# The feed-forward input's two float16 halves: made from rows in SBUF and turned by DMA transposes, in place of TensorE transposes through PSUM

## What is computed

```python
x = _layernorm(x + attn(x), axis=-1)        # x: (4, 512, 512)
x = _layernorm(x + ffn(x), axis=-1)

def ffn(x):                                 # w1, w2: (1408, 512), w3: (512, 1408)
    x1 = x @ quantize(w1).T
    x2 = x @ quantize(w2).T
    return (sigmoid(x1) * x2) @ quantize(w3).T
```

## Time and profile before

| | us |
|---|---|
| median of 3 runs | 715.89 |
| lowest, highest | 715.37, 715.91 |
| span of the profiled execution | 713.9 |
| TensorE busy | 643.5 |
| VectorE busy | 493.3 |
| ScalarE busy | 352.4 |
| GpSimd busy | 129.6 |

### The profile page before, as it was taken

One profiled execution on the slowest core, in us unless ns is written; L12 is line 12 of the kernel. 1 busy time (PEld: TensorE's weight loads), 2 busy tenths in 40 slices (PEclk: granted clock), 3 DMA queues, 4 the chain that ended last, 5 costly groups with the idle time before them and its releaser, 6 DMA issues.

```text
span 713.9 us, 10940 instructions
## 1 busy us (share of the span) xinstructions
PE 643.5 (90%) x3336; PEld 351.8 (49%) x3336; DVE 493.3 (69%) x816; ACT 352.4 (49%) x814; POOL 129.6 (18%) x147
## 2 busy tenths in 40 slices
PE   6756667569999999999999999999999999997996
PEld 2534445243455655543565655644555565643442
DVE  2857878494887888557887886648887885654333
ACT  2664549251376767421576766411676675403320
POOL 1146450832200030012100210012000300110001
PEclk9686868879999999999999999999999999998999
DMA  7651514001122112002042030012032020010001
GB/s 259 236 184 27 195 29 149 0 1 30 29 54 88 38 43 76 1 34 83 7 119 56 6 90 29 17 49 60 16 105 60 9 51 1 16 45 0 1 1 59
DMA packets 20515, 42.02 MB, mean 59 GB/s; under 512 B 4704, under 2 KB 5856, under 8 KB 19936
## 3 DMA queue, kind: packets, MB, share of 16 engines
q1 hardware_dynamic: 19488, 39.86, 18.5%
q10 hardware_dynamic: 960, 1.33, 0.5%
HBM read 20.20 MB, written 4.19 MB: 34 GB/s over the span
## 4 chain that ended last, share of the span: by engine, by line
PE 69%; DVE 9%; issue 8%; POOL 7%; ACT 5%; DMA 1%; DVEq 0%; POOLq 0%; ACTq 0%
PE t_ps L945 12%; PE a_ps L906 10%; PE b_ps L906 10%; PE c_ps L996 7%; PE a_ps L872 6%; PE s_ps L934 6%; PE a_ps L920 5%; PE b_ps L920 5%; POOL q L374 5%; PE a_ps L893 3%; ACT p_sb L477 2%; ACT q L494 2%; DVE sh_sb L694 2%; PE b_ps L893 1%; DVE pt_sb L701 1%
## 5 line engine op out<-in xcount | busy, mean ns | idle before, releaser
L477 ACT ACTIVATE p_sb<-s_ps,sh_sb 128x512 f32<-128x512 f32 x240 | 164.2, 688 | 125.6 <-DVE sh_sb L694 125.6
L945 PE MATMUL t_ps<-table_sb,p_sb 128*128 128x128 f32 x1024 | 147.2, 289 | 33.3 <-ACT pt_sb L485 24.6
L945 PEld LDWEIGHTS t_ps<-table_sb,p_sb 128*128 128x128 f32 x1024 | 125.7, 149 | 74.8 <-ACT p_sb L477 33.7
L694 DVE TENSOR_REDUCE sh_sb<-s_ps 128x1 f32<-128x512 f32 x240 | 157.7, 680 | 1.0 <-PE s_ps L934 1.0
L701 DVE COPY pt_sb<-t_ps 128x512 f32<-128x512 f32 x128 | 88.1, 688 | 65.4 <-PE t_ps L945 63.2
L485 ACT ACTIVATE pt_sb<-t_ps 128x512 f32<-128x512 f32 x128 | 76.4, 597 | 52.3 <-PE t_ps L945 50.6
L934 PE MATMUL s_ps<-k_st,q_st 128*128 128x512 f32 x240 | 92.7, 472 | 3.1 <-DVE k_st L621 2.5
L906 PE MATMUL a_ps<-late,q 128*128 128x512 f16 x352 | 85.2, 386 | 3.5 <-DVE late L636 3.4
L906 PE MATMUL b_ps<-late,q 128*128 128x512 f16 x352 | 84.0, 382 | 0.0
L872 PE MATMUL a_ps<-xT_sb,wq_sb 128*128 128x512 f32 x128 | 62.5, 620 | 9.2 <-DMA wq_sb<-in_wq 6.3
L996 PE MATMUL c_ps<-pt_sb,v_sb 128*32 128x512 f32 x512 | 61.9, 627 | 6.8 <-DVE pt_sb L701 6.8
(11 more groups left out here) (77 smaller groups left out, 613.8 us busy)
## 6 DMA issues: line engine op xcount, KB each, us to landing
q_st<-hi SPq DMA_DIRECT2D x128, 64.0 KB, 2.0
q_st<-lo SPq DMA_DIRECT2D x128, 64.0 KB, 2.0
late<-in_w SPq DMA_DIRECT2D x2, 2816.0 KB, 11.8
xT_sb<-in_xT SPq DMA_DIRECT2D x8, 512.0 KB, 4.8
late<-in_x SPq DMA_DIRECT2D x4, 1024.0 KB, 5.5
out<-late SPq DMA_DIRECT2D x16, 256.0 KB, 2.0
late<-in_w SPq DMA_DIRECT2D x2, 1408.0 KB, 7.0
wo_sb<-in_wo SPq DMA_DIRECT2D x1, 1024.0 KB, 5.7
```

Source lines behind the costliest of these rows:

```text
L477: act.activation(p_sb[:, h % 2, t, :], score_bank(b, n), ACT.Exp, bias=sh_sb[:, n % (2 * SR):n % (2 * SR) + 1], scale=-1.0, accum_out=sums ...
L694: dve.tensor_reduce(sh_sb[:, n % (2 * SR):n % (2 * SR) + 1], score_bank(b, n), AX.X, ALU.min).then_inc(maxed, 1)
L945: mm = pe.transpose(t_ps[k % 2][:, t * P:(t + 1) * P], p_sb[:, h % 2, t, k * P:(k + 1) * P], id_sb)
```

## The change

ScalarE and VectorE make the two halves of h from h_sb, with the tokens still on the partitions, into hr: the bytes of pt_sb's last slot, seen as float16. ScalarE waits for `normed` and once for the last context of the batch before (`ctx_filled`), which reads that slot. SP then issues two DMA transposes for each token tile, SBUF to SBUF, 128 tokens by 512 features each (128 KB), one for the high and one for the low half, in the order high 0, low 0, high 1 and so on, behind q0's stack in a seam and ahead of the last stores in the tail. Each waits for its half. TensorE makes no transposes of h. Its first `up` of a batch waits for all eight transposes (`hT_in`). The order in which the two PSUM banks are used loses its four entries for h.

```diff
@@ bank_uses
-        uses += [use for use in [f"{stage}{t}" for stage in ("wo", "ht") for t in range(TT)]
+        uses += [use for use in [f"wo{t}" for t in range(TT)]
                  if late_bank(period, use) == bank]
@@ layer
+        hr = pt_sb[:, PTR - 1, :, :].bitcast(F16).rearrange("p t (s d) -> p s t d", s=2)
+        hT_in = sem("hT_in")
@@ sync
+            def turn_h(b, t):
+
+                cols = slice(t * P, (t + 1) * P)
+                sp.wait_ge(h_hi, (b - 1) * TT + t + 1)
+                stand(sp)
+                sp.dma_start_transpose(hT[:, 0, :, cols], hr[:, 0, t, :]).then_inc(hT_in, 16)
+                sp.wait_ge(h_lo, (b - 1) * TT + t + 1)
+                stand(sp)
+                sp.dma_start_transpose(hT[:, 1, :, cols], hr[:, 1, t, :]).then_inc(hT_in, 16)
...
+                if not first:
+                    for t in range(TT):
+                        turn_h(b, t)
                 stack(b, 1)
...
             for t in range(TT):
+                turn_h(B, t)
+            for t in range(TT):
                 store(B - 1, t)
@@ scalar
             def h_high(b, t):
 
-                ps, filled, drained, at = late_tile(b, f"ht{t}")
-                act.wait_ge(filled, at(b, f"ht{t}"))
-                act.activation(hT[:, 0, :, t * P:(t + 1) * P], ps[:, :].rearrange("p (k t) -> p k t", k=DT),
-                               ACT.Copy, scale=H_SCALE).then_inc(h_hi, 1)
+                act.wait_ge(normed, (b - 1) * 2 * TT + t + 1)
+                act.activation(hr[:, 0, t, :], h_sb[:, t, :], ACT.Copy, scale=H_SCALE).then_inc(h_hi, 1)
...
                 if not first:
+                    act.wait_ge(ctx_filled, b * HG)
                     h_high(b, 0)
...
+            act.wait_ge(ctx_filled, B * HG)
             for t in range(TT):
                 h_high(B, t)
@@ vector
             def h_low(b, t):
 
-                ps, filled, drained, at = late_tile(b, f"ht{t}")
                 dve.wait_ge(h_hi, (b - 1) * TT + t + 1)
-                dve.scalar_tensor_tensor(out=hT[:, 1, :, t * P:(t + 1) * P],
-                                         in0=ps[:, :].rearrange("p (k t) -> p k t", k=DT), scalar=H_SCALE,
-                                         in1=hT[:, 0, :, t * P:(t + 1) * P], op0=ALU.mult,
-                                         op1=ALU.subtract).then_inc(drained, 1)
+                dve.scalar_tensor_tensor(out=hr[:, 1, t, :], in0=h_sb[:, t, :], scalar=H_SCALE,
+                                         in1=hr[:, 0, t, :], op0=ALU.mult, op1=ALU.subtract).then_inc(h_lo, 1)
@@ tensor
-            def turn_h(b, t):
-
-                ps, filled, drained, at = late_tile(b, f"ht{t}")
-                pe.wait_ge(normed, (b - 1) * 2 * TT + t + 1)
-                pe.wait_ge(drained, at(b, f"ht{t}") - 1)
-                for k in range(DT):
-                    mm = pe.transpose(ps[:, k * P:(k + 1) * P], h_sb[:, t, k * P:(k + 1) * P], id_sb)
-                mm.then_inc(filled, 1)
...
                 if f == 0 and half == 0:
-                    pe.wait_ge(b_drained, bin_(b, "ht3"))
+                    pe.wait_ge(hT_in, b * TT * 2 * 16)
...
-                    turn_h(b, 0)
                     score(b, 0, 0)
                     project_out(b, 3)
-                    turn_h(b, 1)
                     score(b, 0, 1)
                     score(b, 0, 2)
                     project_q(b, 1, [0, 1])
-                    turn_h(b, 2)
                     project_q(b, 1, [2, 3])
-                    turn_h(b, 3)
                 values(b)
...
             for t in range(TT):
                 project_out(B, t)
-            for t in range(TT):
-                turn_h(B, t)
```

## The result

The changed kernel takes **739.27 us** (median of 4 runs, 738.64 to 741.01) against 715.9 before: 1.0334 times as long, 95% interval 1.0319 to 1.0349. The profiled execution of it has a span of 737.0 us, before 713.9. The time went where the forecast of 738 put it, term by term within 2.2 us.

A forecast was written before the change was run, and what follows sets the result against it. TensorE, busy 90% of the span, bounds the kernel. Seams 9.2 + tail 6.4 + clock 6.6 = 22.2 us on a 713.9 us span gives 736.1; plus 2.0 to the median, 738; range 721 to 775.

The forecast's parts named there:

- The frame: Whole kernel: TensorE's order is the clock, busy 90%; time lost ahead of the heads is not won back there.
- The hold: SP's queue: one transpose holds SP for 1.22 us, the middle in ratio of 0.61 and 2.44.
- dear: Rival, seams and tail: hold 2.44, landing 5.6, 775 us; chance 0.2 together with times between forecast and this.
- The landing: Seams and tail: last transpose lands 2.6 us after its issue; bounds 2.0 and 5.6.
- A seam: Between two batches: last transpose lands at 196.2, `up` 3.1 us after 193.13; three seams make 9.2.
- The halves: Seam: ScalarE and VectorE make them from SBUF at no cost, the last low half ready at 191.6.
- whole possible gain of a seam: Seam: without the turns of t=2 and t=3, TensorE could begin `up` 1.6 us earlier, were the data there.
- The tail: After the last batch: seven transposes queue behind the low half of t=0, last landing 654.9 against 648.50, loss 6.4 us.
- The clock: Seams: falls to 0.50 during 4.7 us of idleness, 2.2 us each, 6.6 in three; the tail has paid already.
- As cheap as a copy: Rival, seams and tail: hold 0.61, landing 2.0; 721.3 us if the clock holds, 727.9 if not; chance 0.14.
- Faster: Rival, seams and tail: gain at a landing under 0.65 us; 710.7 us with hold and landing nothing; chance 0.03.
- no difference: Rival, whole kernel: within 1.4 us of nothing for a landing of 0.3 to 1.0 us; chance 0.03.

The follow-up runs named there:

- experiments 4 and 5: Changed kernel with both halves of a tile in one 128x1024 transpose, 737.13 us; with each transpose cut into two of 128x256, 778.51 us.
- experiment 2: Changed kernel with each DMA transpose replaced by a plain copy of the same bytes in the same 256-byte runs, result not turned: 730.89 us.
- experiment 1: Changed kernel without its eight DMA transposes, `up` waiting only for the low halves and reading other data, result wrong: 712.78 us.
- experiment 6: Changed kernel with unread TensorE matmuls ahead of the first `up`, 5 in a seam and 14 in the tail: 731.63 us.
- experiment 3: Changed kernel with the same eight transposes issued in the order in which their halves become ready: 738.98 us.
- experiment 7: Kernel before with the change made in the tail alone, TensorE's turns kept in the three seams: 723.87 us.

## Why the prediction was right, point by point

**The frame held.** TensorE's gaps set the time, the loss is what the seams and the tail lost, and the heads gave nothing back beyond 0.64 us.

**The hold: the right value for the wrong reason.** I took 1.22, the middle between a copy and four blocks' worth. It is 1.20, with 1.31 from start to start. But it is no middle: experiments 4 and 5 show a fixed price for each instruction, from 256 to 1024 columns. That the value fits is luck. The step "as much as a copy for each of its four blocks" was no real bound, and had the change turned wider or narrower pieces, my value would have missed by the factor. With it the rival "dear" falls.

**The landing:** 2.6 forecast, 2.4 measured in the trace, and 2.54 from the last issue to `up`. That it would be above 2.0 for its 512 runs was right: plain copies in such runs land in 2.3 (experiment 2).

**A seam:** 3.1 us forecast, 3.75, 3.77 and 3.89 measured. In seam 1 low 1 goes out at 188.28, which is 188.98 in the times of before (this seam began 0.70 earlier), 0.3 later than the 188.7 that I used. The four starts behind it take 5.36 us, 1.34 each, where the forecast has 4.9, another 0.46. Both are the mis-sized terms; I counted the hold of an instruction and not the distance between starts.

**The halves, and what a seam could gain.** I had the last low half ready at 191.6 at no cost. It is ready at 191.30, which is 192.00 in the times of before, 0.4 late. The DMA path hides that, but it is why the "whole possible gain of a seam" is 1.0 us and not 1.6: in experiment 1, without the DMA path, `up` still waits 0.31 us for this half.

**The tail:** 6.4 forecast, 6.84 measured. Six starts at 1.31 make 7.84 in place of 7.3; the landing gives 0.1 back.

**The clock:** 6.6 forecast, 6.5 measured in the seams, and 7.6 us of the whole time disappear when TensorE is kept busy in the seams and the tail (experiment 6). That "the tail has paid already" was right as well: third there is 5.30 in place of 5.64. The single falls cost 1.99 to 2.48, and up to 2.9 in experiment 3, so the good agreement of the sum has some luck in it: I had put the same 2.2 on each fall, while in seam 1 of experiment 3 the price went with how much of the low stretch lay over the `up` matmuls.

**As cheap as a copy:** refuted in its hold and its landing. The rival's times of 721.3 and 727.9 would also have been too low for copies: experiment 2 has 730.9, since a copy of 512 short runs lands in 2.3, its starts stand 0.7 to 0.8 us apart and not 0.61, and the clock falls in 3.57 us of idleness and the matmuls behind it. The Trainium skill (Advanced Engine Details and Errata, X-Bar Transpose) has transposing DMAs as fast as regular ones. At 128 KB the measurement decides against it for the issue (1.20 us of SP in place of 0.59) and nearly for it for the landing (2.4 against 2.3); the whole difference is 8.4 us of this kernel's time. The Trainium skill (VectorE: DVE Perf Modes, The three transpose paths) gives 1309 ns for one block of 128x128 by DMA. No hold or landing of these runs has that value. The distance between two starts comes near it, but for whole transposes of two and four blocks alike (1.31 us), so these rows don't bear it out as a price of one block.

**Faster, no difference:** a landing under 0.65 us was needed, and 2.4 was measured. Experiment 1, with neither hold nor landing, gave 712.8 where I had worked out 710.7, since a seam gained 0.8 to 1.0 and not 1.4.

**What would show it:** transposes 1.2 us apart (1.31), some 5 us of idleness ended by a DMA (5.07), values over at about 191.5 (191.11, or 191.81 in the times of before), a clock of 0.50 for some 4 us (about 6 to 7 us, from the microsecond of 194 to that of 201, and 5 us of it with TensorE at work): each is in the rows above.

## What to carry to other kernels

By the prices measured here a DMA transpose in place of a TensorE transpose can pay only where its result is wanted several microseconds later; no run here shows such a place. Count one start (1.3 to 1.4 us) on the issuing queue for each instruction, nearly the same from 256 to 1024 columns, then the landing (2.3 to 3.2 us), from the moment the last data are ready, and put the sum on TensorE's idle time with the clock's fall on top. Where a TensorE transpose stands in the way because of its bank, look for an idle bank and another place in the order first: here that took 0.4 to 1.0 us off each place, and with the clock kept in the tail 0.6 to 0.8% of the time. Where a wait of several microseconds can't be avoided, unread matmuls into an idle bank kept the clock at 1.00.

## What was not expected of the hardware

A transpose held SP for 1.17 to 1.25 us (medians) with 256, 512 and 1024 columns alike, while its landing went from 2.3 over 2.4 to 3.2 us.

The low clock cost more after a shorter idle time (experiment 3: 4.31 us idle, third 7.31; the change: 5.07 and 6.89). In seam 1 its fall and its return moved with the moment at which TensorE ran out of work, not with the moment at which `up` began. This is read from two traces and was not tried by itself.

GpSimd's smallest operation got slower beside VectorE's new low half, which reads and writes SBUF alone. In the seam of the change:

```profile
181.07 0.22 POOL L399 TENSOR_SCALAR rstd<-mv 128x1 f32<-128x1 f32 x1 [4.88 <-DVE mv L678]
...
183.66 0.46 POOL L399 TENSOR_SCALAR rstd<-mv 128x1 f32<-128x1 f32 x1 [1.71 <-DVE mv L678]
```

The second ran beside the low half of 183.38, and took 0.46 us in place of 0.22; so did the next, at 187.81, beside that of 187.53. In experiment 7, where the low half of the seams reads PSUM as before, both take 0.22. The 0.24 us go into the norm of tile 1 and from there into low 1, which explains most of the 0.3 us by which low 1 was late. That the two coincide was seen in every seam; the cause was not tested by itself. It isn't this one VectorE instruction alone: in the kernel before, the same GpSimd operation took 0.55 us at 175.67, beside VectorE's `rot` operation of 175.38 (line 604, 0.74 us), which reads and writes SBUF alone as well. In all these rows the GpSimd operation ends about 0.1 us after VectorE's: 184.12 after 184.04, 188.27 after 188.19, 176.22 after 176.12. So it looks as if it waited for VectorE's end rather than ran more slowly; that reading is not tested either.
